# Summing the L1 messages of a graph network by feature instead of by node: ScalarE stages the gathered rows

## The reference

```
h = relu(x @ W_node + b_node)
edge_weight = sum(z * edge_attr, axis=1)
for i in range(3):
    m = h @ conv_weight[i]
    agg = segment_sum(edge_weight[:, None] * m[src], dst)
    h = gru_cell(agg, h, w_ih, w_hh, b_ih, b_hh)
return h
```

## Time and profile before

| | us |
|---|---|
| median of three runs | 6666.83 |
| the profiled execution | 6669.71 |
| its span, first to last instruction | 6667.9 |
| POOL busy | 4813.1 (72%) |
| VectorE busy | 3763.7 (56%) |
| PE busy, matmuls | 3315.7 (50%) |
| ScalarE busy | 875.1 (13%) |
| gathers, 3928 of `h_rows` on POOL | 3751.6 busy, 955 ns each |

### The profile page before, as it was taken

How to read it: one execution, slowest core, us unless ns; L and a number is a source line. 1 busy time by engine, 2 the same in 40 slices (tenths; PEclk the granted TensorE clock), 3 DMA queues, 4 the chain that set the end, 5 groups by cost and what they waited for, 6 DMA issues and landing times.

```text
span 6667.9 us, 87916 instructions
## 1 busy us (share of the span) xinstructions
PE 3315.7 (50%) x13560; PEld 2689.4 (40%) x13561; DVE 3763.7 (56%) x13397; ACT 875.1 (13%) x2172; POOL 4813.1 (72%) x5075
## 2 busy tenths in 40 slices
PE   3444445444447455545755554596444444444444
PEld 3333334333334444544444443333333333333333
DVE  6666665666666656656566664444454445343334
ACT  1000002000002111111311110143333333000000
POOL 6777776777773777777777777665777775777775
PEclk5555556555557676676776665697555555555556
DMA  5333332333332222222122222244222222121112
GB/s 142 107 106 104 105 107 71 73 74 74 73 74 50 52 53 53 53 53 53 44 52 52 53 53 53 56 186 148 52 51 52 52 52 53 52 53 52 53 52 58
DMA packets 259678, 468.33 MB, mean 70 GB/s; under 512 B 91761, under 2 KB 164690, under 8 KB 253155
## 3 DMA queue, kind: packets, MB, share of 16 engines
q0 software_dynamic: 158800, 311.43, 19.2%
q10 hardware_dynamic: 35040, 73.87, 3.5%
q1 hardware_dynamic: 65587, 80.28, 3.4%
HBM read 389.97 MB, written 77.27 MB: 70 GB/s over the span
## 4 chain that ended last, share of the span: by engine, by line
POOL 45%; DMA 19%; issue 17%; PE 13%; DVE 4%; ACT 1%; DVEq 0%; POOLq 0%; SPq 0%; ACTq 0%
POOL G L577 44%; DMA G<-h_rows,ix_src 17%; PE ps L678 12%; DMA G<-t_rows,pos 1%; POOL by_src L601 1%; PE ps L737 0%; DVE HNA L1135 0%; DVE M L1115 0%; DMA t_rows<-G 0%; DVEq L1124 0%; DVE bst L1052 0%; DVE gate L1518 0%; ACT G L1772 0%; DVE X L1135 0%; ACT HNA L1594 0%
## 5 line engine op out<-in xcount | busy, mean ns | idle before, releaser
L577 POOL DMA_INDIRECT G<-h_rows,ix_src x3928 | 3751.6, 955 | 1313.8 <-issue 1052.6
L678 PE MATMUL ps<-G,M 128*128 x10000 | 2551.2, 420 | 3177.4 <-SPq L501 2372.0
L678 PEld LDWEIGHTS ps<-G,M 128*128 128x128 f32 x10000 | 2161.6, 308 | 3528.2 <-issue 3520.6
L1135 DVE TENSOR_TENSOR HNA<-HNA,ps 128x128 f32 (+1 forms) x3328 | 957.7, 288 | 1404.1 <-PE ps L678 1393.9
L1115 DVE TENSOR_SCALAR M<-irow,rel,w_l 128x128 f32<-128x128 f32 x3328 | 1199.4, 364 | 212.2 <-issue 206.3
L577 POOL DMA_INDIRECT G<-t_rows,pos x784 | 749.5, 956 | 265.6 <-issue 227.0
L1135 DVE TENSOR_TENSOR HTA<-HTA,ps 128x129 f32 x840 | 243.4, 290 | 545.9 <-PE ps L678 544.8
L1696 ACT ACTIVATE sorting<-sorting,pk 128x128 f32<-128x128 f32 x784 | 250.6, 390 | 1451.6 <-DVE sorting L1311 1449.1
L678 PE MATMUL ps<-sorting 128*128 128x128 f32 x1568 | 434.4, 374 | 0.9 <-ACT sorting L1696 0.7
L1772 ACT ACTIVATE G<-G,pk 128x128 f32<-128x128 f32 x784 | 314.7, 402 | 688.8 <-DMA G<-t_rows,pos 688.3
L1135 DVE TENSOR_TENSOR X<-X,ps 128x128 f32 x832 | 238.9, 287 | 229.2 <-PE ps L678 228.1
(11 more groups left out here) (258 smaller groups left out, 2186.0 us busy)
## 6 DMA issues: line engine op xcount, KB each, us to landing
G<-h_rows,ix_src POOLq DMA_INDIRECT x3928, 2.5
t_rows<-G SPq DMA_DIRECT2D x49, 1024.0 KB, 3.9
HTA<-in_edge_attr_n ACTq DMA_DIRECT2D x50, 500.0 KB
HTA<-in_edge_attr ACTq DMA_DIRECT2D x50, 500.0 KB
sorting<-q_flat ACTq DMA_DIRECT2D x98, 196.0 KB, 3.3
G<-t_rows,pos POOLq DMA_INDIRECT x784, 2.5
h_rows<-HS SPq DMA_DIRECT2D x30, 256.0 KB
h_rows<-HNA SPq DMA_DIRECT2D x24, 256.0 KB
```

The lines of the kernel that those rows point to most:

```text
L577: return nc.gpsimd.indirect_dma_start(to, None, table, bass.IndirectOffsetOnAxis(ap=ix, axis=0))
L678: return nc.tensor.matmul(dst, lhsT, rhs, start=start, stop=stop, skip_group_check=True)
L1135: V.tensor_tensor(to, to, ps[:, u % SLOTS, 0:n], ALU.add).then_inc(s_add, 1)
```

## The change

In the three L1 passes the roles of the two operands of the matmul are exchanged. ACT copies the slot of G of each step into a ring of four fixed tiles `Gs` and counts `s_gs`; it does the register reads and the arrival waits that the PE did, and waits until the matmul four steps back is done. The PE takes `Gs` as weights and M as the moving operand, so the product has features on the partitions. The sums lie in `sumT` (the storage of HNA, 128 columns per block), and POOL's credit in these passes is `s_gs`. The GRU stages read `sumT` directly: the transposes of the sums, the aT copy and the PE's wait for it go. The zeroing becomes `clean`, placed after the sigmoids and before the tanh. ACT's other work in the passes is issued between its copies: a `Qb` load every eight steps, the scaling of a quad (`number`) one quad ahead, at the step of a quad's last tile, and the copy of a chunk (`ordered`) in the following chunk or behind the pass.

```diff
+        sumT = HNA[:, :, :].rearrange("p t c -> p (t c)")[:, 0:NP]
+        Gs = sb("Gs", [P, GS, D])
...
                     if t % 4 == 0 and t + 3 >= RING:
-                        pool.wait_ge(s_mm, k * S + t + 3 - RING + BLK)
+                        if k in L1_PASSES:
+                            pool.wait_ge(s_gs, (k - PASS_L1) * S + t + 3 - RING + BLK)
+                        else:
+                            pool.wait_ge(s_mm, k * S + t + 3 - RING + BLK)
...
+            def round_by_feature(k, r, extra=None):
+                for u in range(RD):
+                    s = r * RD + u
+                    pe.wait_ge(s_add, k * S + s + 1)
+                    pe.wait_ge(s_m, k * S + s + 1)
+                    pe.wait_ge(s_gs, (k - PASS_L1) * S + s + 1)
+                    mm(ps[:, u % SLOTS, 0:P], Gs[:, u % GS, :], M[:, u % MR, :]).then_inc(s_mm, 1)
+                    if extra:
+                        extra(r, u)
...
-                    pe.wait_ge(s_a2, b("a2", ph) + i + 1)
-                    mm(bank(0, i), wc[:, l, 0:D], of(aT, i), start=False).then_inc(s_a3, 1)
+                    mm(bank(0, i), wc[:, l, 0:D], sums(i), start=False).then_inc(s_a3, 1)
...
-                    unrolled([(0, gru_in), (0, gru_gates), (1, gru_back)])
+                    unrolled([(0, gru_gates), (1, gru_back)])
...
-                args = (HNA, D, rel, w_l, b_i)
+                args = (sumT.rearrange("p (t d) -> p t d", d=P), D, rel, w_l, b_i)
...
+            def by_step(k, beside):
+                for r in range(NRD):
+                    _, at_g = nc.values_load_multi_w_load_instructions(
...
+                    for u in range(RD):
+                        s = r * RD + u
+                        if u % QUAD == 0:
+                            act.wait_ge(s_arr[k], upto[u // QUAD])
+                        act.wait_ge(s_mm, k * S + s + 1 - GS)
+                        A.copy(Gs[:, u % GS, :],
+                               G[:, bass.ds(at_g[u], 1), 0:D].rearrange("p t d -> p (t d)")).then_inc(s_gs, 1)
+                        beside(r, u)
...
+                if u % PB == 3 and 0 <= j < PLACES:
+                    if j >= 2:
+                        act.wait_ge(s_pl, j - 1)
+                    act.dma_start(Qb[:, j % 2, :], q_of[j:j + 1, :].broadcast_to((P, PB * BLK))) \
+                        .then_inc(s_qld[j % 2], 16)
...
+            def number(j):
+                act.wait_ge(s_lo, j + 1)
+                for k in range(B4):
+                    to = lo_m[:, j % 2, k, :]
+                    ins = A.mul(to, to, pk[:, j * B4 + k:j * B4 + k + 1])
+                ins.then_inc(s_low, 1)
...
+                if v < NB and t % B4 == B4 - 1 and j + 1 < ET // B4:
+                    number(j + 1)
+                if v0 < v < NB and t % TB == 5:
+                    ordered(v - 1)
...
+                def clean(i):
+                    act.wait_ge(s_a3, b("a3", ph) + 3 * i + 3)
+                    A.copy(sums(i), zf[:, 0:1].broadcast_to((P, tiles(i) * P))).then_inc(s_zero, 1)
...
-                    unrolled([(0, copy_in(ph)), (1, keep), (0, gates_rz), (0, gate_n)])
+                    unrolled([(1, keep), (0, gates_rz), (0, clean), (0, gate_n)])
```

More of the change, by code:

```diff
@@ L52 @@
 SLOTS = 4
+GS = 4
 W1 = D + 1
@@ L350, in gnn_kernel @@
         s_mm = sem("s_mm")
+        s_gs = sem("s_gs")
         s_add = sem("s_add")
@@ L416, in feat, with sums @@
             return HT[:, bass.ds(g * GN * P, tiles(g) * P)]
+        def sums(g):
+            return sumT[:, g * GN * P:(g * GN + tiles(g)) * P]
         def of(t, g):
@@ L438, in gnn_kernel @@
         PARTS = ((0, 4), (4, 10), (10, 16))
+        L1_PASSES = range(PASS_L1, PASS_L1 + LAYERS)
         N_LOADS = 25
@@ L699, in one_round, with pass_by_feature @@
                         extra(r, u)
+            def round_by_feature(k, r, extra=None):
[7 more added lines that the diff above has]
+                        extra(r, u)
+            def pass_by_feature(k, r0, r1, extra=None):
+                with rounds(pe, r0, min(r1, FEED)) as r:
+                    round_by_feature(k, r, extra)
+                for r in range(max(r0, FEED), r1):
+                    round_by_feature(k, r, extra)
             def gather_pass(k, r0, r1, n, extra=None):
@@ L1666, in step @@
                         return
-                    elif not (isinstance(i, int) and i == 0):
-                        act.wait_ge(s_a3, b("a3", ph) + 3 * i)
-                    A.copy(of(aT, i), bank(4, i)).then_inc(s_a2, 1)
-                    if ph in (G0, G1, G2):
-                        A.copy(group(HNA, i), zeros.broadcast_to((P, tiles(i), W1))).then_inc(s_zero, 1)
+                    raise ValueError(ph)
                 return step
@@ new lines, in number, with ordered, order @@
+            def number(j):
[4 more added lines that the diff above has]
+                ins.then_inc(s_low, 1)
+            def ordered(v):
+                act.wait_ge(s_pm, 1 + (v + 1) * (TB // B4))
+                A.copy(chunks[:, v, :], ps[:, 6 + v % 2, 0:P]).then_inc(s_part, 1)
+            def order(v0, r, u):
+                t = tile_at(r % HALF * RD + u)
+                if t is None:
+                    return
+                v = v0 + r // HALF * 2 + t // TB
+                j = v * (TB // B4) + t % TB // B4
+                if v < NB and t % B4 == B4 - 1 and j + 1 < ET // B4:
+                    number(j + 1)
+                if v0 < v < NB and t % TB == 5:
+                    ordered(v - 1)
@@ L1708, in _ @@
                     act.dma_start(q_flat.rearrange("(b p h) -> p b h", p=TB, h=BLK), Q).then_inc(s_qst, 16)
[L1709 to L1722 removed]
+                    by_step(PASS_L1 + l, spread)
+                else:
+                    v0, v1 = PASS_ORDER[PASS_L1 + l]
+                    if v0 == 0:
+                        number(0)
+                    by_step(PASS_L1 + l, lambda r, u, v0=v0: order(v0, r, u))
+                    ordered(v1 - 1)
+                def clean(i):
+                    act.wait_ge(s_a3, b("a3", ph) + 3 * i + 3)
+                    A.copy(sums(i), zf[:, 0:1].broadcast_to((P, tiles(i) * P))).then_inc(s_zero, 1)
                 def gates_rz(i):
```

54 lines of the change are left out of this document (18 added, 36 removed), and 4 rows, old and new, of the table per.

## The result

The changed kernel takes 6677.89 us (median of 20 runs, 6674.16 to 6681.48), the kernel before 6669.11 (20 runs, 6663.70 to 6672.53): ratio 1.0014, 95% interval 1.0008 to 1.0020. It became slower by 9 us, where I had forecast 2 us faster. The profiled execution took 6677.62 us (span 6675.8), 7.9 more than that of before. The table cuts the time at the gathers of `h_rows`: a pass runs from its first gather's start to its last one's, and a gap over a GRU stage from the last gather before it to the first behind it. The last column has what the prediction said each would gain or lose.

A forecast was written before the change was run, and what follows sets the result against it. POOL's issue of gathers was taken to bound the passes, left unchanged. Pass ends +0.7, G0 +1.3, G1 +0.8 and G2 -4.5 sum to -1.7: profiled 6668.0, median 2.9 lower, so 6665 us; range 6657 to 6675, with rivals 6656 to 6684.

The forecast's parts named there:

- G2: Last GRU stage: transposes go and zeroing moves, -4.5 us in all, bounds -10.5 and +1.5.
- eight table steps: In G2 from step 4 on: HNA transposes of 0.44 us go from each step, zeroing hides, -3.5 us.
- the first four: G2's steps 0 to 3: step 0 +0.1, clock rising as before; steps 1 to 3 -1.0 together.
- the pass's end: Last burst waits for a copy first: 0.35 us each into G0 and G2, +0.7 together, bounds 0.2 and 1 each.
- the open size: TensorE's clock in G2: eight table records take 3.89 or 5.40 us, four times each; changes cost 1.5 us each.
- G0: First GRU stage: the gate loop overtakes PE's pace, 0.28 us slower per pair of groups; +1.3, bounds -1.5 and +2.6.
- G1: Second GRU stage: scaling ahead of the last chunk copy delays POOL's first scatter; +0.8 us, bounds 0 and +3.
- 2.3 us in hand: In G1: the GRU path's slack behind POOL's scatters, expected to absorb its own +1.3 and +0.35 us.
- The passes: Three L1 passes: ScalarE's copies and other jobs stay covered, the number of gathers sets the price; cost 0.
- rival 2: L1 passes: ScalarE's stream stalls the ring past 11 steps; 39 us, 6704, mild forms 6680 to 6690; chance 7%.
- Rival 1: L1 passes: ScalarE's traffic slows the gathers, 2496 copies adding 52 us, total 6717; chance 4%.
- Rival 3: Stages gain the removed work: G0 -1.5, G1 0, G2 -10.5, gathers 7 us shorter; 6646 to 6655; chance 4%.

The follow-up runs named there:

- f3: Kernel after with the 52 transposes of the sums back on TensorE in G2, unread: 6679.6 us, ratio 1.0016 to the kernel before.
- f1: Kernel after with two unread 128x512 products in the chunk-copy wait of each G2 table step: 6671.8 us, ratio 1.0006 to the kernel before.
- g3: f4 plus unread products in the waits of G2's first four steps and near each L1 pass's end: 6669.2 us, ratio 0.9982 to the kernel before.
- g4: f6 plus the same added products in the same places as g3: 6669.4 us, ratio 0.9984 to the kernel before.
- f2: Kernel after with the zeroing behind the tanh in all three GRU stages: 6675.2 us, ratio 1.0009 to the kernel before.
- f6: Kernel before with two unread 128x512 products in the wait of eight G2 table steps: 6664.0 us, ratio 0.9993 to the kernel before.
- g1: Kernel before plus ScalarE's copies in the three L1 passes, which PE awaits but does not read: 6690.1 us, ratio 1.0014 to the kernel before.
- j1: g1 with copies of 8 columns instead of 128: 6675.3 us, ratio 1.0009 to the kernel before.
- i1: Change in third L1 pass and G2 only, zeroing behind the tanh, waits filled as in g3, rest as before: 6655.4 us, ratio 0.9976 to before.
- g2: Kernel after with every ScalarE copy issued twice, the first unread: 6698.0 us, ratio 1.0027 to the kernel before.
- f4: Kernel after, zeroing behind the tanh, scaling past the pass's end deferred, eight G2 table waits filled: 6664.8 us, ratio 0.9994 to the kernel before.
- series e and h: Two series of follow-up runs with late gather landings, each timed beside the kernel before, which took 8402.8 and 8375.2 us there.
- h3: Kernel after, unchanged, run with late landings: 8455.4 us, ratio 1.0107 to the kernel before.
- h1: Same kernel as i1, run with late landings: 8402.7 us, ratio 1.0037 to the kernel before.
- h2: Same kernel as g4, run with late landings: 8382.8 us, ratio 1.0013 to the kernel before.

## Why the prediction was wrong

**G2, the step that failed.** It said -3.5 for eight table steps, about -0.9 for the first four, and put the slow bursts at bounds of -10.5 and +1.5 in all. With the +0.35 of the pass's end that is -4.1 over the gap; it became +5.8, beyond the upper bound. The terms, from the two profiles:

- The end of the pass: +0.4, as forecast.
- The first four groups, from the first PE work of the stage to the fourth group's transposes back: 48.52 us in place of 46.08, +2.4 for -0.9. The transposes of HNA gave back 3.5 and the zeroing cost 2.1 (0.52 each). But the twelve gate records of a group took 8.48 us against 6.73 in the first group and 29.84 against 25.59 over the four, +4.3, because more of them ran at 1.2 GHz. I had let the clock rise "at the same moment as before" in the first group and given it no term in the others.
- The first table step: its first eight records took 5.87 us in place of 3.79, +2.1. This had no term.
- The eight steps behind it: -3.5 came (0.44 in each), and slow bursts went from four to seven, +4.5.

I had named the clock the open size of the table steps and then centred on "no change", as if taking PE's work away were neutral to it. It was not: with the work put back unread the slow bursts are four again and the steps take no longer (f3), with the wait filled there is none (f1), and with the waits filled in both kernels the change gains 5.6 (g3 against g4). That removed work must always cost clock is not shown; it did in this stage.

**G0** gave +1.6 against +1.65 over the gap, and that agreement is partly luck. The reason was right: f2 takes the loss off by moving the zeroing. The size was not: from the second group to the last the stage lost 3.0 us, where I had +1.4 for five pairs. The start gained 1.2 where I had +0.35 for the later burst and -0.1. Nor is the gap itself better known than that. It is 92.4 to 93.0 us in f6, g1, g4 and j1 with the old stage, 95.25 in the profile of before and 95.09 in i1. In before the last copy out waited 4.11 us for a store, in f6 2.55, and the first group took 7.48 us against 6.71.

**G1**, +1.4 against +0.8. The first scatter came 1.3 us later, not 0.8, but the scatters did not decide: I left the GRU chain 2.3 us in hand and gave it 1.65 of loss. It lost 4.3: 3.0 in the groups, as in G0, 0.9 in the first group, whose first products ran at 1.2 GHz (3.12 us for four records, 1.88 before), and 0.4 at the start. So the next gather waited 1.26 us for the last store:

```profile
3266.64 0.99 POOL L586 DMA_INDIRECT G<-h_rows,ix_src  x1 [1.26 <-DMA h_rows<-HS]
```

f6, whose G1 is as before, has a gap of 95.01 against 94.41, so the 1.4 is known to half a microsecond or so.

**The passes**, 0 forecast. ScalarE had the reserve that I gave it, and rival 2 (its stream holds the ring) never showed. Rival 1 said that the traffic lengthens the gathers, by 52 us: refuted in size by every pass, and as a mechanism by j1 and the sorted gathers of the first pass. But I had written that long gathers follow VectorE's wide work and that this shifts, took it as noise of 7 us either way, and counted it at nothing. It is 3.0 us in the first pass (mean of five with the change, 984.3, against 981.3 of two; the profiled pair alone +1.5; 4.3 between g4 and g3) and 2.7 by the same count in the second, where g4 and i1 make it less sure. **Rival 3** was half right: the removed work was worth 5.6 us in G2, to a kernel that holds the clock and zeroes behind the tanh.

What stays open: depending on which profiles with and without the change are compared, the three passes cost 2 to 7 us, G0 1 to 4, G1 0 to 2 and G2 1 to 6. That sums to 4 to 19 us, against 9 measured, while the profiled execution has 7.9, with 3 us less in the L0 pass that did not change. Executions differ by that much.

## What to carry to other kernels

Work taken off TensorE is not a gain until the waits beside it are looked at: ask what the engine does between the removed work and its next wait, and whether the work behind that wait already starts at the lower clock. A copy put ahead of a matmul shifts what stands behind the matmul, and where VectorE's wide work coincides with longer issues of POOL, as here, a shift of 0.2 us under a stream of 784 of them can cost microseconds although the copy itself costs POOL nothing. When a forecast of a stage comes true, check its terms one by one: G0 hit its total with two errors of over a microsecond that cancelled. Where a change gains in one layer and loses in the others, try it in that layer only.

## What the runs showed of the hardware

- Behind a wait of 1.92 us PE started the next burst at 1.2 GHz in four of eight steps with the transposes in them (24.66 and 23.16 us long; before, f3, g1, j1), in six or seven of eight without them (24.22 and 22.72 us; after, f2, g2), and in none when 1.7 of the 1.92 us were filled with products that nobody reads (f1, f4, f6). A slow burst of eight records costs 1.5 us.
- Filling waits with unread products made the kernel before faster, 0.9984 (0.9975 to 0.9993) in g4, where nothing else was touched; f1 against the kernel after has 1.0006 and 1.0014, with overlapping intervals.
- Gathers of POOL took 0.945 us on average with a ScalarE copy over them and 0.956 to 0.981 under VectorE's wide two-operand work. The wide product of two SBUF operands ran while a gather began in 9 to 24 of 98 places without the copies and in 74 to 91 with them.
- In series e and h gathers landed late: the 65th gather of the L0 pass came 52 us after the 64th, L1 passes took 1.19 to 1.26 ms, and in h the unchanged kernels took 8375 (before) and 8455 us (after, ratio 1.0107). The view of lines for h3 shows POOL waiting for slots that ScalarE (`Gs`) and PE (`ps`) had not yet set free:

```profile
L586 POOL DMA_INDIRECT G<-h_rows,ix_src x3928 | 3761.0, 957 | 2629.3 <-issue 1120.9 <-ACT Gs L1723 745.3 <-PE ps L690 424.9
```

  Why the change costs 80 us there and 9 elsewhere was not settled; in h1, with copies in the third pass only, that pass took 1242 us against 1192 in h2.
